# Windowed attention: the division of the head outputs moves from VectorE to ScalarE and GpSimd

## What is computed

```python
qkv = x @ W_qkv + b_qkv                    # 16 heads of 8
scores = einsum('bnid,bnjd->bnij', q, k) / sqrt(8)
mask = (diff < 0) | (diff >= 32)           # a window of 32 keys
attn = softmax(where(mask, -inf, scores))
out = einsum('bnij,bnjd->bnid', attn, v)
x = x + (out @ W_out + b_out)              # of layernorm(x)
x = x + moe(layernorm(x))                  # top-1 of 7 experts and "none", plus a shared expert
```

## Time and profile before

| | us |
|---|---|
| median of 3 runs | 327.05 (326.39 to 329.93) |
| the profiled execution | 329.34 |
| its span, first to last instruction | 327.6 |
| busy: PE, DVE, ACT, POOL | 298.1, 224.7, 147.3, 175.0 |
| attention loop, first to last row maximum | 16.9 to 130.2 |

### The profile page before, as it was taken

One profiled execution on the slowest core, in us unless ns is written; L12 is line 12 of the kernel. 1 busy time (PEld: TensorE's weight loads), 2 busy tenths in 40 slices (PEclk: granted clock), 3 DMA queues, 4 the chain that ended last, 5 costly groups with the idle time before them and its releaser, 6 DMA issues. The chain is left out here.

```text
span 327.6 us, 11893 instructions
## 1 busy us (share of the span) xinstructions
PE 298.1 (91%) x4834; PEld 244.8 (75%) x4834; DVE 224.7 (69%) x438; ACT 147.3 (45%) x230; POOL 175.0 (53%) x277
## 2 busy tenths in 40 slices
PE   8899999999799897999983489999989999999994
PEld 8646676576566474678872378888989999999994
DVE  6699999898588797777961153466558778775442
ACT  3434556444344673782720012253345555556530
POOL 7797585723127652910277604444438666764344
PEclk9999999999799999999995589999999999999999
DMA  7961422414041422099412201114244544343320
GB/s 194 349 157 48 111 57 85 105 52 108 20 118 47 109 51 62 5 395 335 133 52 104 102 0 68 66 66 75 58 80 85 99 82 89 67 97 79 76 52 26
DMA packets 52504, 32.47 MB, mean 99 GB/s; under 512 B 25424, under 2 KB 46676, under 8 KB 52450
## 3 DMA queue, kind: packets, MB, share of 16 engines
q1 hardware_dynamic: 47968, 23.18, 28.7%
q0 software_dynamic: 2880, 6.43, 5.6%
q10 hardware_dynamic: 1602, 2.10, 2.0%
HBM read 13.72 MB, written 11.95 MB: 78 GB/s over the span
## 5 line engine op out<-in xcount | busy, mean ns | idle before, releaser
L682 POOL DMA_INDIRECT out<-y,xn_base x38 | 39.6, 1041 | 37.7 <-DVE y L1366 35.4
L777 ACT ACTIVATE Pr<-psS 128x1024 f32<-128x1024 f32 x32 | 32.8, 1025 | 31.3 <-PE psS L1472 31.3
L1114 DVE TENSOR_TENSOR hT<-psS,PT 128x512 f32<-128x512 f32 x32 | 22.3, 696 | 34.9 <-remote 11.9
L859 ACT ACTIVATE PT<-psS 128x512 f32<-128x512 f32 x32 | 19.0, 597 | 55.3 <-PE psS L1606 47.9
L1351 DVE TENSOR_TENSOR Pr<-psS,PT 128x512 f32<-128x512 f32 x38 | 26.0, 685 | 23.4 <-PE psS L1745 9.9
L963 DVE TENSOR_REDUCE row_max<-psS 128x16 fp32r<-128x1024 f32 x32 | 37.7, 1218 | 4.8 <-PE psS L1460 4.7
L892 ACT ACTIVATE PT<-psS 128x512 f32<-128x512 f32 x38 | 22.7, 597 | 39.5 <-PE psS L1735 16.9
L1733 PE MATMUL psS<-xT_hi,taken_parts 128*128 128x256 f32 x128 | 38.5, 301 | 0.0
L1018 DVE STREAM_TRANSPOSE PT<-Pr 128x1024 f32<-128x1024 f32 x32 | 37.3, 1205 | 0.0
L649 POOL DMA_INDIRECT sorted_rows<-rows,pos_u x24 | 23.0, 959 | 25.4 <-DVE rows L1119 19.0
L1734 PE MATMUL psS<-xT_lo,taken_parts 128*128 128x256 f32 x128 | 36.1, 282 | 0.0
(11 more groups left out here) (223 smaller groups left out, 681.3 us busy)
## 6 DMA issues: line engine op xcount, KB each, us to landing
sorted_rows<-pad_rows SPq DMA_DIRECT2D x9, 528.0 KB, 5.3
xn_base<-sorted_rows SPq DMA_DIRECT2D x38, 66.0 KB
rows<-in_L_attn_x SPq DMA_DIRECT2D x8, 256.0 KB, 6.5
xs<-sorted_rows SPq DMA_DIRECT2D x64, 32.0 KB
VD_even<-V SPq DMA_DIRECT2D x28, 72.0 KB
VD_odd<-V SPq DMA_DIRECT2D x28, 72.0 KB
w_sb<-in_L_ffn_w_gate ACTq DMA_DIRECT2D x1, 1792.0 KB, 11.8
Kx<-K SPq DMA_DIRECT2D x28, 64.0 KB
```

The source lines that it names most:

```text
L682: pool.indirect_dma_start(out=out_list, out_offset=bass.IndirectOffsetOnAxis(tok_u[:, r, :], 0), in_=y[:, r, :], in_offset=None, bounds_ch ...
L777: nc.scalar.activation(Pr[:, half, :], psS[:, half, :], ACT.Exp, scale=SCALE).then_inc(exp_done, 1)
```

## The change

For pairs 0 to 13 (BY_POOL = NP - 2 = 14), ScalarE copies the weighted values and denominators from PSUM to a new SBUF tile `heads`, between the two exponentials of the next turn. VectorE takes the reciprocals from that copy, between the two transposes of the probabilities. GpSimd multiplies, behind the rest of its turn. VectorE transposes the heads behind the second transpose of the probabilities. `weigh_values` waits for the copy in place of the multiplication. Pairs 14 and 15 stay as they were.

```diff
+    BY_POOL = NP - 2
+        heads = sb("heads", [P, TPP, NH * VW])
@@ GpSimd @@
+            def divide_heads(p):
+                pool.wait_ge(heads_taken, p + 1)
+                pool.wait_ge(rden_done, p + 1)
+                if p > 0:
+                    pool.wait_ge(ot_done, p)
+                for t in range(TPP):
+                    o = heads[:, t, :].rearrange("q (h j v) -> q h j v", j=NJ, v=VW)
+                    r = rden[:, t, :].rearrange("q (h j) -> q h j", j=NJ)
+                    last = pool.tensor_tensor(
+                        On[:, t, :].rearrange("q (j h d) -> q h j d", j=NJ, d=HD), o[:, :, :, 0:HD],
+                        r.unsqueeze(3).to_broadcast([P, NH // NJ, NJ, HD]), ALU.mult,
+                    )
+                last.then_inc(on_done, 1)
...
+            divide_heads(0)
             for p in range(EARLY):
                 residual(p)
...
                 if p == SPLITS + 1:
                     split(up_sb, shared_in[0], up_hi, up_lo)
+                divide_heads(p + 1)
                 if h == 1 and b + 2 < B:
                     add_bias(b + 2)
             moments(0, G1, st2_done, G1)
             deviations(0, G1 // 2)
             residual(EARLY)
+            divide_heads(EARLY + 1)
             deviations(G1 // 2, G1)
             shifts(0, G1, norm2_ready)
             add_bias(B - 1)
             normalise_rows(0, 1)
             residual(EARLY + 1)
+            divide_heads(EARLY + 2)
             normalise_rows(1, 1)
             normalise_rows(2, 1)
             residual(EARLY + 2)
+            divide_heads(EARLY + 3)
             residual(EARLY + 3)
@@ ScalarE @@
+            def evict_heads(p):
+                act.wait_ge(pv_done, (p + 1) * TPP)
+                if p > 0:
+                    act.wait_ge(on_done, p)
+                nc.scalar.copy(heads[:, :, :], psO[:, :, 0 : NH * VW]).then_inc(heads_taken, 1)
...
                 exponentials(p, 0)
                 if p in (0, 2):
                     evict_xnT(n)
+                if 0 < p <= BY_POOL:
+                    evict_heads(p - 1)
                 exponentials(p, 1)
@@ VectorE @@
+            def sums_of_taken(p):
+                dve.wait_ge(heads_taken, p + 1)
+                if p > 0:
+                    dve.wait_ge(on_done, p)
+                o = heads[:, :, :].rearrange("q t (s v) -> q t s v", v=VW)
+                nc.vector.reciprocal(rden[:, :, :], o[:, :, :, HD]).then_inc(rden_done, 1)
...
-                if p > 0:
+                if p > BY_POOL:
                     output(p - 1)
-                else:
+                elif p == 0:
                     input_stats(3, stats1_done)
                 turn_probs(p, 0)
+                if 0 < p <= BY_POOL:
+                    sums_of_taken(p - 1)
                 turn_probs(p, 1)
+                if 0 < p <= BY_POOL:
+                    turn_heads(p - 1)
                 if p + 4 < B:
                     input_stats(p + 4, stats1_done)
@@ TensorE, weigh_values @@
                     pe.wait_ge(pt_done, (p + 1) * HALVES)
-                    if p > 0:
+                    if 0 < p <= BY_POOL:
+                        pe.wait_ge(heads_taken, p)
+                    elif p > 0:
                         pe.wait_ge(on_done, p)
```

More of the change, by code:

```diff
@@ L246, in windowed_attention_top1_moe_kernel @@
         rden_done, on_done, ot_done = sem("rden_done"), sem("on_done"), sem("ot_done")
+        heads_taken = sem("heads_taken")
         op_done, proj_ready = sem("op_done"), sem("proj_ready")
```

## The result

| us | before | after |
|---|---|---|
| median of 4 runs each, same chip | 326.72 (325.75 to 329.93) | 338.11 (337.18 to 338.9) |
| the profiled execution | 329.34 | 337.4 |
| its span | 327.6 | 335.7 |

The ratio is 1.0292 with a 95% interval of [1.0232, 1.0352]: slower by 11.4 us in the medians, by 8.1 in the two spans. Ratios leave out slow executions, those more than 1.5% above the fastest of the same kernel.

A forecast was written before the change was run, and what follows sets the result against it. The loop was taken as bound by waits for TensorE's scores, not VectorE. GpSimd's queue stalls (7.35), with clock +0.9 and gaps -0.9 cancelling, gave +7.4: 327.05 + 7.4 = 334.4 us, range 330.5 to 339.5.

The forecast's parts named there:

- round 1 to 2, behind `add_bias`: GpSimd busy until 30.3 delays multiplication and `turn_heads`; round 2 starts at 32.35, not 30.74: +1.6.
- round 2 to 3, behind the constants: GpSimd's constants end at 38.4 and the multiplication follows: round 3 starts at 40.5, not 38.33; sum so far +2.2.
- rounds 3 and 4: GpSimd finishes residual, moments, or normalisation and split about when the reciprocals are done: +0.1.
- round 5, behind moments and split: GpSimd's residual, second moments and split end at 61.9, `turn_heads` about 63.2, not 58.78: +4.4 so far.
- late `project` in round 6: After round 5's stall, `project` starts behind `turn_heads` and not with the scores: another 0.25.
- the clock in round 6: TensorE idles 2.2 before round 6, then may run at 1.2 GHz: between 0 and 1.5, taken +0.9.
- rounds 11 to 13, late residual: Multiplications push GpSimd's work back; residual 11 ends at 118.5 instead of 115.15, delaying VectorE's moments: +2.1.
- round 14, `turn_rows`: TensorE's `turn_rows(1)` waits for GpSimd's work behind `divide_heads(12)`: 0.45, and 0.15 for `project`'s later start, +0.6.
- gaps without releaser: TensorE's own gaps, 5.1 in 5 times, may shrink through idle time elsewhere: between 0 and -5.1, taken -0.9.
- The shared port: VectorE transposes in two-port mode could lock out GpSimd's multiplication, some 0.8 a round; the forecast said the trace speaks against.
- the second rival: Shift mostly swallowed: gaps without releaser vanish (-5.1 instead of -0.9) or later stages absorb: +3, 330.2; chance 0.08.
- The first rival: VectorE's relief pays in the attention loop: 14 x 0.53 = 7.4 gained, 319.6; chance 0.03.

The follow-up runs named there:

- before again: The kernel before, with no edit, run again on a second chip: 0.9989 [0.9952, 1.0025], 311.25 us.
- after again: The changed kernel, with no further edit, run again on a second chip against the kernel before: 1.0226 [1.0195, 1.0258], 318.09 us.

## Why the prediction was right

Slower was right, and 338.11 lies inside the range (330.5 to 339.5), 3.7 above the 334.4. The mechanism, GpSimd's in-order queue, is the forecast's; part of the nearness is not its merit, as the terms behind the queue show. By its steps:

| step of the sum | forecast | measured |
|---|---|---|
| round 1 to 2, behind `add_bias` | +1.6 | +1.63 |
| round 2 to 3, behind the constants | +0.6 | +0.37 |
| rounds 3 and 4 | +0.1 | +0.33 |
| round 5, behind moments and split | +2.1 | +2.01 |
| late `project` in round 6 | +0.25 | +0.24 |
| the clock in round 6 | +0.9 | +1.1, with a gap of 0.72 gone: +0.63 with the row above |
| rounds 11 to 13, late residual | +2.1 | +2.05 |
| round 14, `turn_rows` | +0.6 | +0.76 |
| gaps without releaser | -0.9 | -0.1 in sum, but see below |

**The queue.** Its steps sum to 7.35 in the forecast and to 7.4 in the rows above. Round by round, before again and after again give 7.8 (2.37, 0.40, 0.35, 1.64, 0.34, 2.18 and 0.50); the whole kernel cost 7.0 there by its ratio, 6.1 to 8.0 by the interval. The waits of `turn_heads` were called at 1.5, 1 and 2 us and are 1.87, 0.78 and 2.21.

**The durations.** The multiplication was taken at 0.9 a pair from rows of another shape, and took 0.77; the strided operand cost nothing that its bound of 1.25 had allowed for. ScalarE's copy took 396 ns for the forecast 0.40, at no cost.

**The shared port.** The Trainium skill's rule (SBUF — State Buffer, section "SBUF: two separate sides") was weighed and put aside. In after the two engines ran side by side, in VectorE's timeline and GpSimd's row of 115.10 above:

```profile
114.89 1.19 DVE L1049 STREAM_TRANSPOSE PT<-Pr 128x1024 f32<-128x1024 f32 x1
```

The multiplication started 0.2 into the transpose and took 0.78, no more than elsewhere; the transpose took its 1.19. Nothing was locked out in this pairing. One engine holding up the other does show in this study, but where VectorE divides from the copy itself: its multiplication of two SBUF tiles took up to 1.39 in place of 0.45 beside GpSimd.

**The clock.** Granted clock of after, two windows behind the stall of round 5 (busy us of PE, PEld, DVE, ACT, POOL, then PEclk, DMA share, GB/s):

```profile
64.00:66.00 2.00, 2.00 (x66) 1.27 (x55) 1.59 (x4) 0.20 (x1) 1.72 (x4) 0.50 0.37 80
66.00:68.00 2.00, 2.00 (x68) 1.69 (x68) 0.72 (x1) 1.63 (x3) 0.75 (x2) 0.77 0.40 94
```

TensorE's timeline of after behind the stall, then of before in the same round:

```profile
63.01 0.79 PE L1552 MATMUL psB<-wout_sb,OT 128*128 128x128 f32 x4 [1.88 <-DVE OT L1078]
...
64.84 1.22 PE L1514 MATMUL psS<-row_max,minus_ident 128*128 128x512 f32 x2
```
```profile
60.06 0.70 PE L1472 MATMUL psS<-row_max,minus_ident 128*128 128x512 f32 x2
...
62.13 0.26 PE L1492 MATMUL psO<-VD_even,PT 128*32 128x36 f32 x5 [0.72 <-issue]
```

TensorE had idled 1.88 before `project`, and then stood at 0.50 (1.2 GHz). From `project` to the products of the next batch it took 4.58 (63.01 to 67.59), in before 4.19 (58.67 to 62.86) with a gap of 0.72 in it, so 3.47 of work: the clock cost 1.1, near the 0.9 taken. Only 0.63 show in the round, because the gap was gone. On the second chip the same stall was 1.34 long on TensorE, the clock stayed at 1.00, and the gap was there, 1.40.

**The gaps.** The term of -0.9 failed: in sum the gaps stayed at 5.0 (7.0 on the second chip). That takes the second rival's footing away. One gap did go, the 0.72 of round 6, in the stretch in which TensorE ran at half clock. And 1.68 came off between rounds 9 and 10: 0.33 by a shorter gap, 1.38 by the clock, which in before's profiled execution had dropped behind its gap of 2.13 and did not drop in after or in before again. So the two unknown terms, which the forecast let cancel at +0.9 and -0.9, came out at +1.1 for the clock in round 6 and -0.1 for the sum of the gaps.

**The sum.** Of the 11.4 us between the medians the two profiles show 8.1: 7.4 of queue, 1.1 of clock, less 0.7 and 1.7 as just told, less 0.2 by which after's loop starts earlier, and 2.2 behind attention. The other 3.3 are the difference of the profiled executions from their medians, and no profile shows what they are. That the forecast lies 3.7 under the median comes from there and from behind attention, not from the queue.

**The first rival** had the sign wrong for a reason that the runs give more sharply than the forecast did: VectorE's 6.9 us were worth nothing that could be measured. The forecast still granted them a value in the rounds with `input_stats`.

**What the forecast did not see** is the stretch behind attention. It expected the shift unchanged to the end. The shift was 6.0 up to the cast of `tile_at` (193.54 before, 199.54 after), and 8.1 at the next residual (196.11 and 204.25). Those 2.1 us are not of the queue's making in attention, and they are not in the second chip's profiles: there the shift is 8.90 at the cast and 8.90 at the residual.

## What to carry to other kernels

Moving work to an idle-looking engine helps only if the engine that it leaves sets the pace: here the waits for the scores already said that it did not, and leaving the work out altogether gained nothing. In an in-order queue the price of a hand-off is not the duration of the work handed over (0.77 us) but what stands ahead of it, so add up the queue's turn by turn ends against the moment in which the result is needed. And when work is moved out of the way, look up who waits for its semaphore: three kernels here lost 2.9 us behind attention by constants that were moved without it. A control can bring a cost of its own: the division on VectorE, from the copy, was held up by GpSimd in three rounds, which the change itself never met.

## What the runs showed of the hardware

**Waits during GpSimd's indirect DMAs, on one chip only.** While GpSimd issues the scatter (`DMA_INDIRECT`, 0.96 each with 0.30 between), VectorE's `hT` of the shared expert waited on the first chip, in both kernels. The profile names `remote` as the releaser of some of these waits. VectorE's timeline of before, then of after:

```profile
175.40 0.69 DVE L1114 TENSOR_TENSOR hT<-psS,PT 128x512 f32<-128x512 f32 x1 [6.24 <-remote]
...
186.60 0.69 DVE L1114 TENSOR_TENSOR hT<-psS,PT 128x512 f32<-128x512 f32 x1 [5.65 <-remote]
```
```profile
181.42 0.69 DVE L1156 TENSOR_TENSOR hT<-psS,PT 128x512 f32<-128x512 f32 x1 [6.34 <-remote]
...
187.66 0.69 DVE L1156 TENSOR_TENSOR hT<-psS,PT 128x512 f32<-128x512 f32 x1 [4.96 <-remote]
...
196.04 1.43 DVE L1156 TENSOR_TENSOR hT<-psS,PT 128x512 f32<-128x512 f32 x2 [7.69 <-remote]
```

Those put down to `remote` add to 11.9 in before and 19.0 in after, but that is a matter of the label: with those ahead of the two `hT` between and behind, at 180.26 (3.58) and 190.78 (3.49), which it puts down to TensorE and ScalarE, the waits ahead of the same four `hT` add to 19.0 in before as well. The label hides that ScalarE stood still too: in before it was idle for 12.25 ahead of 178.13, although the gate products that its activation reads had ended at 170.2. TensorE was granted 0.50 of its clock meanwhile, here in before:

```profile
174.00:188.00 14.00, 6.51 (x14) 4.22 (x15) 2.67 (x4) 1.19 (x2) 9.88 (x11) 0.50 0.29 106
```

On the second and third chips no wait for `remote` stands in any profile, and the granted clock of after again is 1.00 from 170 to 190. Most of the 16 us between the chips lies here: before's last round of attention starts at 129.03 on the first chip and at 128.10 on the second, its cast of `tile_at` at 193.54 and at 175.59. After's 2.1 us more there are a matter of order: its last two `hT` ran together at 196.04, so that TensorE's next six products (196.79 to 199.51, at half clock) stood ahead of the down products, where in before they had run ahead of the last `hT` (187.35 to 190.28). What holds the engines in these waits the trace doesn't show, and no run here settled it.

**Gaps with no releaser** on TensorE, in the value products, sum to 3.9 to 7.0 us in every kernel of this study. They are not scattered: in the 14 profiles they stand at eight places of the program only, ahead of the last 5, 7, 8, 19, 21, 35, 39 or 55 of a tile's 64 matmuls, and each place belongs to one round. The one ahead of the last 7 is in every profile, 0.48 to 2.16 long.

The trace holds what ends them. Among the DMA queues one carries instructions, in packets of 16 KB. The queues of before from 81.8 to 83.6, its line for this one (packets, MB, share of 16 engines):

```profile
q8 instruction: 1, 0.02, 6.0%
```

That packet ran from 81.83 to 83.56, and the gap of 2.13 ended at 84.93, 1.37 later. In before again the packet landed at 83.44 and the gap ended at 84.61, in after at 87.90 and 89.19, in after again at 88.45 and 89.78. In all 84 gaps of the 14 profiles the end comes 1.2 to 1.6 us after such a packet has landed. So TensorE waits there for its own instructions; no run here changed the fetching, and this reading rests on the times alone. It also tells why idle time elsewhere did not close the gaps, and why the half clock closed one: in round 6 of after the packet landed at 65.53, and TensorE came to the place only at about 67. For the waits of the first topic it is no answer: in before no packet of an instruction queue lies between 169 and 203.
